# Cross-attention kernel: the lower halves of the memory rows made on GpSimd and not on VectorE

## What is computed

```python
memory_proj = memory @ W_mem.T                       # (1601, 512) per batch
scores = x @ memory_proj.T / sqrt(512)
attn = softmax(scores)
memory_context = attn @ memory_proj
gate = sigmoid(concat([x, memory_context]) @ W_gate.T + b_gate)
fused = x + gate * memory_context
out = fused / sqrt(mean(fused**2) + 1e-6) * norm_w
```

## Time and profile before

| | |
|---|---|
| time, three runs | 561.19 us median (560.53 to 563.08) |
| the profiled execution | 562.44 us, its span 560.6 us |
| PE busy | 541.7 us, 97%, 2432 matmuls |
| VectorE busy | 503.4 us, 90% |
| ScalarE busy | 336.2 us, 60% |
| GpSimd busy | 134.1 us, 24% |
| mean granted TensorE clock | 0.992 of full speed |

### The profile page before, as it was taken

The page is one execution under the profiler, slowest core; times in us unless marked ns, Lnnn a source line. Parts: engine busy times, 40 slices in busy tenths (PEclk is TensorE's granted clock), DMA queues, the critical chain, the costliest instruction groups (busy, mean ns, idle before and its releaser), DMA issues.

```text
span 560.6 us, 9004 instructions
## 1 busy us (share of the span) xinstructions
PE 541.7 (97%) x2432; PEld 438.8 (78%) x2432; DVE 503.4 (90%) x847; ACT 336.2 (60%) x633; POOL 134.1 (24%) x102
## 2 busy tenths in 40 slices
PE   8999999999999999999999999999999999999992
PEld 7777888878887788878888788887888778887871
DVE  4879959999899998899998998999988999889966
ACT  4676646665567646576366665666565864667534
POOL 0005600244003520055001440025300451005600
PEclk9999999999999999999999999999999999999988
DMA  9965371520683117711385115841088212100033
GB/s 226 260 127 83 90 132 50 98 73 18 148 176 97 37 50 136 167 68 37 98 163 104 56 37 134 171 114 40 0 170 177 75 37 99 52 23 20 0 114 112
DMA packets 184338, 54.25 MB, mean 97 GB/s; under 512 B 161528, under 2 KB 174848, under 8 KB 184320
## 3 DMA queue, kind: packets, MB, share of 16 engines
q1 hardware_dynamic: 183792, 53.52, 40.9%
q10 hardware_dynamic: 528, 0.52, 0.3%
HBM read 45.63 MB, written 8.39 MB: 96 GB/s over the span
## 4 chain that ended last, share of the span: by engine, by line
PE 66%; DVE 17%; issue 10%; SPq 3%; ACT 2%; DMA 2%; ACTq 0%; DVEq 0%
PE bank L357 14%; PE bank L358 13%; PE bank L359 13%; PE bank L524 7%; PE bank L525 7%; PE bank L526 7%; DVE p_lo L838 5%; DVE s L879 3%; DVE fused L984 2%; DVE fused L991 2%; DVE gate L905 2%; ACT fused L696 2%; DVE gate L934 2%; DMA fused<-in_L_xattn_W_gate_dram 2%; SPq L249 2%
## 5 line engine op out<-in xcount | busy, mean ns | idle before, releaser
L1155 POOL TENSOR_TENSOR psum_rows<-psum_rows,p_tmp 128x512 f32<-128x512 f32 (+1 forms) x88 | 122.5, 1392 | 85.4 <-ACT p_tmp L673 84.3
L838 DVE TENSOR_TENSOR p_lo<-p_tmp,p_hi 128x512 fp32r<-128x512 f32 (+1 forms) x104 | 92.3, 889 | 5.5 <-ACT p_hi L635 5.4
L673 ACT ACTIVATE p_tmp<-s 128x512 f32<-128x512 f32 (+1 forms) x104 | 65.2, 628 | 45.1 <-DVE s L879 44.5
L1155 POOL TENSOR_TENSOR psum_rows<-p_tmp 128x512 f32<-128x512 f32 x8 | 10.8, 1354 | 309.4 <-ACT p_tmp L673 309.4
L357 PE MATMUL bank<-q_hi,mt_hi 128*128 128x512 f32 (+1 forms) x208 | 81.7, 393 | 0.0
L358 PE MATMUL bank<-q_lo,mt_hi 128*128 128x512 f32 (+1 forms) x208 | 81.2, 390 | 0.0
L359 PE MATMUL bank<-q_hi,mt_lo 128*128 128x512 f32 (+1 forms) x208 | 81.1, 390 | 0.0
L525 PE MATMUL bank<-p_lo,mem_hi 128*128 128x512 f32 (+1 forms) x208 | 81.0, 389 | 0.0
L524 PE MATMUL bank<-p_hi,mem_hi 128*128 128x512 f32 (+1 forms) x208 | 81.0, 389 | 0.0
L526 PE MATMUL bank<-p_hi,mem_lo 128*128 128x512 f32 (+1 forms) x208 | 80.9, 389 | 0.0
L635 ACT ACTIVATE s<-bank 128x512 f32<-128x512 f32 (+1 forms) x104 | 62.0, 597 | 19.5 <-PE bank L359 19.1
(11 more groups left out here) (93 smaller groups left out, 1057.6 us busy)
## 6 DMA issues: line engine op xcount, KB each, us to landing
mem_raw<-in_ctx_dram SPq DMA_DIRECT2D x48, 256.0 KB, 3.0
mem_blocks<-in_ctx_dram SPq DMA_DIRECT2D x64, 136.0 KB
x_again<-in_x_dram SPq DMA_DIRECT2D x32, 256.0 KB, 2.6
out_dram<-fused SPq DMA_DIRECT2D x32, 256.0 KB, 2.1
x_raw<-in_x_dram SPq DMA_DIRECT2D x112, 64.0 KB, 2.1
mem_blocks<-in_ctx_dram SPq DMA_DIRECT2D x56, 64.0 KB, 2.0
x_raw<-in_x_dram SPq DMA_DIRECT2D x4, 256.0 KB, 4.7
gate<-in_L_xattn_W_gate_dram SPq DMA_DIRECT2D x2, 512.0 KB, 6.1
```

Source lines behind the costliest of these rows:

```text
L673: nc.scalar.activation(p_tmp[0:r, t % TMP_RING, :], s[0:r, t, :], ACT.Exp, scale=float(D) ** -0.5).then_inc(exp_done, 1)
L838: return nc.vector.tensor_tensor(dst, src, hi.bitcast(F32), ALU.subtract)
L1155: nc.gpsimd.tensor_tensor(psum_rows[0:r, :], a, p_tmp[0:r, t % TMP_RING, :], ALU.add).then_inc(p_added, 1)
```

## The change

`mem_lo_part` leaves VectorE and is issued by GpSimd, as a subtraction of the same operands in the same pieces (two tiles of 128x256 each, and 65x256 for the last). GpSimd makes the first six pieces (twelve tiles) of a batch before its first row-sum addition of that batch, each as soon as its upper half is there, and the seventh behind the row-sum addition of t = 5. Everything that waits for `mem_has_lo` is as before.

```diff
-            def mem_lo_part(b, p):
-
-                dve.wait_ge(mem_has_hi, MP * b + p + 1)
-                ts, raw, r = mem_pair(p)
-                lo_part(mem_lo[0:r, ts, :], mem_raw[0:r, raw, :], mem_hi[0:r, ts, :]).then_inc(mem_has_lo, 1)
-
...
-                    for q in SPLIT_BY_SCORES.get(p, []):
-                        mem_lo_part(b, q)
...
-                        for q in SPLIT_BY_SOFTMAX.get(t, []):
-                            mem_lo_part(b, q)
...
+            def mem_lo_part(b, p):
+
+                pool.wait_ge(mem_has_hi, MP * b + p + 1)
+                ts, raw, r = mem_pair(p)
+                nc.gpsimd.tensor_tensor(mem_lo[0:r, ts, :], mem_raw[0:r, raw, :], mem_hi[0:r, ts, :].bitcast(F32),
+                                        ALU.subtract).then_inc(mem_has_lo, 1)
+
...
-            for t in range(1, MT):
-                add_p(0, t, True)
+            def iteration(b, first):
+                for p in range(MP - 1):
+                    mem_lo_part(b, p)
+                for t in range(1, MT):
+                    add_p(b, t, first)
+                    if t in SPLIT_BY_SOFTMAX:
+                        mem_lo_part(b, MP - 1)
+
+            iteration(0, True)
             with pool.Fori(1, B) as b:
-                for t in range(1, MT):
-                    add_p(b, t, False)
+                iteration(b, False)
```

## The result

The changed kernel takes 563.60 us (median of 16 runs, 562.53 to 566.83), the kernel before 561.64 us (16 runs beside them): the ratio is 1.0034, with a 95% interval of 1.0019 to 1.0049. It is slower by 2 us, where 0.6 us of gain was forecast. The profiled execution took 562.58 us with a span of 560.7 us. That span is within 0.1 us of the one before, although the kernel is 2 us slower: the profile before holds the stretch at the lower clock, which this one does not. From its last row sums (L459) to its end it took 24.48 us, 1.7 us more than the second profile of the same kernel, `e0_before`, which has no such stretch.

The account below looks back on a forecast made before the run. TensorE's matmuls were taken as the pace outside two gate waits for VectorE. First batch +0.25, middle batches -0.4 and last batch -0.45 made -0.6 us: 561.8 from the profiled execution, 560.6 from the median; range 557.2 to 563.6.

Parts of the forecast that it names:

- -2.4 to +0.8: Whole kernel: the forecast's own spread in us, said to come from the bounds of its terms.
- TensorE is the pace, and relief of VectorE in the scores wins nothing: Scores: TensorE has no idle time, so a faster VectorE could win only at two waits for bias additions.
- Price of a piece, 1.39 us: GpSimd: a large subtraction costs 1.39 us (1.29 to 1.80), like its addition; the small one 0.7 to 1.39.
- up to 0.7 us: Softmax: VectorE loses up to this where the small piece delays GpSimd's next row-sum addition; no net effect expected.
- So a VectorE operation with two SBUF inputs and a GpSimd one with two exclude each other: Blocking rule: the two take turns; in the scores only the running maximum, 12 a batch, was thought affected.
- half a us earlier: After the last maximum in middle batches: reciprocal, first gate input and ScalarE's first tanh come this much earlier.
- My term was -0.4 us for seven batches: Gate entry: an earlier tanh gains at most 0.05 us a batch, between 0 and 0.8 in all.
- The last maximum: End of scores: piece 3 holds it until 230.9, it ends at 231.6, TensorE wants it at 231.77; no cost.
- The slower rival: End of scores: piece 4 precedes the last maximum, TensorE waits 1.2 us in eight batches, 9.6 us, 570.8; chance 0.11.
- First batch +0.25: First batch's scores: the last maximum ends at 38.1, 0.25 us late for TensorE; between 0 and 0.7.
- Last batch -0.45: Last batch: u_lo starts earlier and shortens TensorE's 0.40 us idle; gain 0.45 us, between 0.2 and 0.6.
- The slow clock: Last batch after the u_lo wait: 3.5 us at 1.2 GHz; shorter idle might save 1.75 us, left out of the sum.

Follow-up runs that it names:

- e0_before: The kernel before the change, run again unaltered for a second profile: 561.63 us, ratio 0.9996.
- the experiment on it: The changed kernel with the halving of the reciprocals given one operand in PSUM, nothing else altered: 562.87 us, ratio 1.0010 to the kernel before.
- e3_maxima_first: The changed kernel with GpSimd's pieces 2, 3 and 4 waiting by semaphore for running maxima 9, 11 and 12: 564.34 us, ratio 1.0042 to the kernel before.

## Why the prediction was wrong, point by point

- **The forecast, -0.6 us, had the wrong sign; +2.0 was measured.** The median of 563.6 lies on the upper end of the range given (557.2 to 563.6). The spread "-2.4 to +0.8" does not follow from the bounds, which add up to -1.4 to +0.5 us, and to -3.15 with the slow stretch.
- **TensorE is the pace, and relief of VectorE in the scores wins nothing:** right. TensorE has no idle in the scores after the change, and both gate waits stayed. But VectorE was to fall below 500 us of busy time and rose to 505.8: the blocking took back all that the move freed.
- **Price of a piece, 1.39 us:** right; 1.46 on average, 1.29 undisturbed, in spite of the rounding. The small one took 1.18 us of the 0.7 to 1.39, of which it spent about half waiting for `p_lo`. The "up to 0.7 us" that its delay of the next row-sum addition costs VectorE came out as 0.70.
- **"So a VectorE operation with two SBUF inputs and a GpSimd one with two exclude each other":** true and incomplete, and this is the first step that failed. The rule asked for two SBUF inputs; the halving of the reciprocals has one, and is held all the same, for 0.88 us. I did not even list it, though it stands in the path that I said starts "half a us earlier": the reciprocal does start 0.7 us earlier, the first gate product 0.14 us later. My term was -0.4 us for seven batches; it came to +0.92 in six of them, of which the experiment on it takes away 0.09 a batch. The rest is 0.03 us in the scores and some 0.02 ahead of the gate. My bounds for this term, 0 to 0.8 us of gain, had no loss in them.
- **The last maximum, "0.2 us is left, cost zero":** right in six middle batches, wrong in the last. I laid one batch in order and took all eight for it. The second failed step, and with 1.3 us of the 2.0 the larger, is the order of the ninth maximum and piece 2, with 0.08 us between them, which I did not list as a margin at all. The slower rival named the right wait, the right engine and nearly the right price (1.2 against 1.27 us), but a wrong trigger and all-or-nothing repetition.
- **First batch +0.25:** L432 starts 0.30 us behind the last transpose there instead of 0.11, so 0.2 us were lost. By the prediction's own figures it should have been 0.4 (36.17 + 1.39 + 0.69 = 38.25 against 37.85); the last maximum came second to piece 3, as laid out.
- **Last batch -0.45:** right, 0.42 us from the row sums to the end.
- **The slow clock:** by the mean clocks it comes in some three of ten executions of the kernel before (32 of 105) and in 1 of 16 of the changed one. The guess that the shorter idle spares it fits these counts. In a median it weighs little, and it was rightly kept out of the sum.

## What to carry to other kernels

Moving elementwise work to GpSimd need not relieve VectorE: each piece here gave VectorE 0.6 us and took about as much back from a later operation with its operands in SBUF, down to a 128x4 one. List every VectorE operation in the window by where its operands lie, the tiny ones too, and follow each into the chain that the critical engine waits for. Where two queues meet within 0.1 us, count the order as undecided, read the gaps in each unrolled copy of the loop by itself, and price the worse order by a kernel that forces it. A change that has a good and a bad part is worth splitting: the one small piece alone was 0.9981, the six large ones alone 1.0060. And the mean granted clock of every execution can tell how often a stretch at the lower clock occurs, where a profile shows it once.

## What the runs showed of the hardware that I had not expected

- A 128x4 `tensor_scalar` from SBUF to SBUF on VectorE, usually 0.17 us, lasted 1.05 us beside a GpSimd subtraction; as `scalar_tensor_tensor` with its second operand in PSUM it took 0.16.
- Between a maximum and a large piece that met within 0.1 us, the one that was issued first went first, in every profile; 0.03 us between the issues decided it in the last batch. Of the three maxima behind it, the last two were then held by pieces 3 and 4 (1.64 and 1.58 us).
- Turns are not always taken. L978, issued at 251.72 while the small piece was ending (251.79), came second to the row-sum addition issued at 251.75. But a maximum that had waited 0.6 us behind piece 3 went in ahead of piece 4.
- GpSimd's piece of 65x256 shows 1.17 to 1.29 us, but it waits for VectorE's `p_lo` in that. In batch 3 `p_lo` ends at 251.20 and the piece at 251.79: about 0.6 us is its own work, by this estimate, against 1.29 for one of 128x512.
- With pieces 2 to 4 released by semaphore (e3_maxima_first), the last maximum ended 0.44 us later than with the pieces already issued and waiting.
- The longer TensorE's wait in the last batch, the more executions show the lower mean clock: 2 of 98 at 0.2 us, 36 of 121 at 0.4, 32 of 43 at 1.0 to 1.5.
